# Two-block graph attention on one core: normalised rows split in SBUF and transposed by DMA, maxima on TensorE, merged aggregation jobs, new step orders

## The chip, the cores and the metric

The kernel runs on one core of a Trainium2 chip. The metric is the device time of one execution in microseconds, the median of several. One execution of the same program was also recorded by the hardware profiler; its span, from the first to the last instruction, is what the trace shows.

## The reference

For each of 32 graphs (256 nodes, 384 features, a boolean adjacency matrix) two residual blocks are computed:

```
h = relu(layernorm(x)); x = x + attention6(h, adj)      # 6 heads of 64, scores q k' / 8, masked softmax, @ Wf + bf
h = relu(layernorm(x)); x = x + gat12(h, adj)           # 12 heads of 32

gat12: hv = h W;  s = tanh(hv) w_src;  d = tanh(hv) w_dst
       p = softmax(mask(leaky_relu(s_n + d_m)));  o = elu(p hv + b);  g = sigmoid(h H_w' + H_b)
       result = g * o + (1 - g) * h
```

Everything is float32 to the outside.

## The kernel before

Every engine has its own list of steps in `ORDERS`, written out by hand as text, and `walk` goes through that list once per iteration n. A step has a letter for its lag: L works on graph n+2, P on n+1, A on n, B on n-1, C on n-2. So five graphs are under way together. Between engines only semaphores order the work, so an engine may run ahead of the iteration that another one is in. SyncE (SP) has a list of its own: it waits in order for what each DMA needs, and then issues it.

The weight matrices and the normalised rows are used as two fp16 parts each (high and low), with three products (`TERMS`). A graph goes through these steps, in the names of the lists:

- STATS0 (VectorE: mean and variance), RSTD0 and NORM0 (GpSimd: the normalised rows `xn`, 128 rows x 2 x 384 in float32).
- LN_T0 (L450): TensorE transposes `xn` in six blocks of 128x128 into two PSUM banks (index 0: four blocks, index 1: two). ScalarE takes the high part out with a Relu (L647), VectorE the low part (L844). The result is `h16`, the features on the partitions.
- Q, K (L476), V (L462): projections. QK (L511): scores; SCORES0 (VectorE, L879): mask and row minimum; EXP0 (ScalarE, L672); NORMP0 (VectorE reciprocal L886, GpSimd product L1076); PT0 (L535): TensorE transposes the probabilities, and ScalarE copies them out (L679). PV0 (L553): aggregation, in three jobs, one for each pair of heads; ScalarE and VectorE take its two fp16 parts (L684, L891). OUT0 (L462, VectorE L899): output projection and residual.
- STATS1, AGGREGATE1, RSTD1, NORM1, LN_T1: the same for the second block. HEADS and GATE (L462; L458 adds a bias in GATE): projections. ScalarE takes tanh (L690) and a copy (L691).
- SCORE_PROD (GpSimd, L1098 twice and L1104), SCORE_SUM (VectorE, L911 to L922), DST_T (L587, VectorE L926): the destination scores as rows. DST (L526) spreads them for two heads, SCALED (ScalarE, L703) multiplies them by 0.2. Twelve units follow: SCORES1 (VectorE, two L945 and two L951 each), EXP1 (ScalarE, L715), PT1 (L535, ScalarE L723).
- PV1 (L597): aggregation in three jobs; VectorE copies each out (L957). OUT_T (L605) transposes back; ELU_BIAS, ELU_RELU, ELU_EXP, FINISH, SKIP_H, GATES, SKIP, OUT_SUM and STORE make and store the output rows.

Jobs share three PSUM banks in turn (`Jobs`). MASK0 and MASK1 turn the loaded adjacency into masks on GpSimd; LOAD_ADJ of a graph waits until MASK1 has read the same buffer two graphs before.

At the start, ScalarE sums each weight's absolute values per partition (L623), GpSimd takes the maximum over the partitions (`partition_all_reduce`, L1009), VectorE makes scales, ScalarE the high part (L627) and VectorE the low part (L778). The sums of four weights stand ahead of the first high part on ScalarE. The bias row of the values is made by fp32 products at the very start (L420).

Of the kernel before, what the change touches and what calls it, by code (L numbers as in the profile page):

```python
# [66 lines left out]
def steps(text):  # L67
# [6 lines left out]
        C PT1 9, A QK 0, B GATE 0, A QK 1, C PT1 10, C PT1 11, B GATE 1, P LN_T0 0, A PT0 0, C PV1 2, B DST_T 0,  # L74
        A QK 2, A PT0 1, C OUT_T 0, P LN_T0 1, B DST 0, C OUT_T 1, A PT0 2, A PV0 0, B DST 1, P Q 0, A PT0 3,
        P K 0, P K 1, A PT0 4, P Q 1, A PT0 5, A PV0 1, A PV0 2, B DST 2, B PT1 0, B DST 3, B PT1 1, A OUT0 0,
        B PT1 2, A OUT0 1, B PT1 3, P Q 2, B DST 4, B PT1 4, P V 0, P V 1, B PT1 5, A LN_T1 0, A LN_T1 1, P K 2,
        B PT1 6, B DST 5, A HEADS 0, A HEADS 1, B PT1 7, B PV1 0, B PT1 8, B PV1 1
    """),
    "ACT": steps("""  # L80
        C PT1 8, C EXP1 10, C PT1 9, C EXP1 11, A EXP0 0, B GATE 0, A EXP0 1, C PT1 10, C PT1 11, B GATE 1,
        P LN_T0 0, A EXP0 2, A EXP0 3, A PT0 0, A PT0 1, P LN_T0 1, B SCALED 0, A EXP0 4, A PT0 2, A PV0 0,
        A EXP0 5, B SCALED 1, P Q 0, B EXP1 0, C ELU_RELU 0, A PT0 3, C ELU_EXP 0, A PT0 4, A PT0 5, B EXP1 1,
        A PV0 1, P Q 1, A PV0 2, B SCALED 2, B EXP1 2, B PT1 0, B EXP1 3, B PT1 1, B PT1 2, B SCALED 3,
        B EXP1 4, B PT1 3, B SCALED 4, B PT1 4, P Q 2, B EXP1 5, P V 0, B EXP1 6, P V 1, A LN_T1 0, A LN_T1 1,
        B PT1 5, B EXP1 7, B SCALED 5, B PT1 6, B EXP1 8, A HEADS 0, A HEADS 1, B PT1 7, B EXP1 9
    """),
    "DVE": steps("""
        C SCORES1 10, C SCORES1 11, C PV1 0, A SCORES0 0, C PV1 1, A SCORES0 1, A NORMP0 0, C RECIP1 0,
        A SCORES0 2, A SCORES0 3, A NORMP0 1, B SCORE_SUM 0, P LN_T0 0, A NORMP0 2, C PV1 2, B DST_T 0,  # L90
        B SKIP_H 0, A SCORES0 4, A NORMP0 3, C OUT_T 0, A SCORES0 5, P LN_T0 1, C OUT_T 1, B SCORES1 0, A PV0 0,
        A NORMP0 4, B SCORES1 1, A NORMP0 5, P K 0, B SCORES1 2, P K 1, C FINISH 0, B SCORES1 3, A PV0 1,
        A PV0 2, C FINISH 1, B SCORES1 4, A OUT0 0, B SCORES1 5, A OUT0 1, A STATS1 0, A STATS1 1,
        A AGGREGATE1 0, B SCORES1 6, L STATS0 0, B SCORES1 7, A LN_T1 0, A LN_T1 1, B SCORES1 8, P K 2,
        B SCORES1 9
    """),
    "POOL": steps("""
        B SCORE_PROD 0, A NORMP0 0, A NORMP0 1, B MASK1 0, A NORMP0 2, A NORMP0 3, C ELU_BIAS 0, P MASK0 0,
        A NORMP0 4, A NORMP0 5, C OUT_SUM 0, B GATES 0, A RSTD1 0, A NORM1 0, L RSTD0 0, P RES_ROW 0, B SKIP 0,
        L NORM0 0  # L100
    """),
    "SP": steps("""
        P LOAD_ADJ 0, L LOAD_X 0, C STORE 0
# [1077 lines left out]
```

## Time and profile before

| | |
|---|---|
| median of 3 runs | 1360.45 us (1359.81 to 1360.91) |
| the profiled execution's own time | 1360.17 us |
| its span | 1358.3 us |
| TensorE busy | 1293.0 us, 95% |
| ScalarE busy | 1252.5 us, 92% |
| VectorE busy | 1213.5 us, 89% |
| GpSimd busy | 903.3 us, 66% |
| mean granted TensorE clock | 0.981 |

The profiled execution lies 0.3 us below the median, and its span 1.9 us below its own time. Busy time is a union over an engine's instructions: neighbouring instructions overlap in the pipeline, so the mean duration of one is longer than the distance from its start to the next one's.

### The profile page before, as it was taken

To read this page: it belongs to the slowest core of one execution; us is meant where nothing else is said; L and a number is where in the kernel's file an instruction comes from. 1 tells how busy PE (TensorE), PEld (TensorE's weight loads), DVE (VectorE), ACT (ScalarE), POOL (GpSimd) and SP (SyncE) were. 2 spreads that over 40 slices of the span, in tenths; PEclk is the share of its full clock that TensorE was granted. 3 is DMA by queue.
4 is the path that set the end of the run, shared out by engine and by line. 5 is a ranking of instruction groups with operands and counts; after the bars stand their busy time and mean duration, and the time that the engine had idled before them with its cause. 6 is when DMAs were issued, how large, how long until landed. Compare 5 with 4: busy or idle time off the path is not lost.

```text
span 1358.3 us, 33510 instructions
## 1 busy us (share of the span) xinstructions
PE 1293.0 (95%) x10502; PEld 905.9 (67%) x10502; DVE 1213.5 (89%) x4457; ACT 1252.5 (92%) x3731; POOL 903.3 (66%) x1106
## 2 busy tenths in 40 slices
PE   2789999999999999999999999999999999999974
PEld 1567677767667776766777676677667677767652
DVE  3569999999999999999999999999999999999885
ACT  4469999999999999999999999999999999999986
POOL 3366676667777667777766777766677776667653
PEclk8899999999999999999999999999999999999997
DMA  4000000000000000000000000000000000000000
GB/s 155 13 14 15 20 20 27 27 27 15 27 17 23 27 27 25 17 27 15 25 27 27 17 26 27 13 27 27 27 16 27 27 13 27 27 26 4 13 13 24
DMA packets 29839, 33.75 MB, mean 25 GB/s; under 512 B 10464, under 2 KB 29664, under 8 KB 29664
## 3 DMA queue, kind: packets, MB, share of 16 engines
q1 hardware_dynamic: 29664, 31.62, 7.4%
q8 instruction: 86, 1.41, 0.4%
q14 instruction: 89, 0.73, 0.2%
HBM read 19.03 MB, written 12.58 MB: 23 GB/s over the span
## 4 chain that ended last, share of the span: by engine, by line
PE 89%; ACT 2%; DVE 1%; issue 1%; POOL 1%; POOLq 0%; DVEq 0%; ACTq 0%
PE job L462 26%; PE pt L535 20%; PE job L476 13%; PE unit L511 7%; PE job L597 7%; PE job L553 7%; PE unit L526 3%; PE job L450 3%; PE job L605 2%; PE job L458 1%; ACT p L715 1%; PE job L587 1%; DVE unit L945 0%; POOL prod L1098 0%; ACT pT L723 0%
## 5 line engine op out<-in xcount | busy, mean ns | idle before, releaser
L715 ACT ACTIVATE p<-y,min 128x256 f32<-128x256 f32 x768 | 396.1, 542 | 1.5 <-DVE min L951 1.4
L535 PE MATMUL pt<-ident,p 128*128 128x128 f32 x2304 | 355.6, 280 | 9.7 <-ACT p L715 5.2
L945 DVE SCALAR_TENSOR_TENSOR unit<-unit,s,dst 128x256 f32<-128x256 f32 x768 | 334.8, 481 | 9.4 <-DVE min L951 0.5
L535 PEld LDWEIGHTS pt<-ident,p 128*128 128x128 f32 x2304 | 265.9, 142 | 86.5 <-issue 43.6
L462 PE MATMUL job<-w,h 128*128 128x384 f16 x1728 | 301.8, 326 | 0.7 <-DVE h L844 0.6
L951 DVE CUSTOM_DVE_ANT_0 y<-unit,mask 128x256 f32<-128x256 f32 x768 | 291.0, 415 | 0.0
L1076 POOL TENSOR_SCALAR p<-p,rec 128x256 f32<-128x256 f32 x384 | 188.3, 507 | 88.3 <-DVE rec L886 82.6
L462 PEld LDWEIGHTS job<-w,h 128*128 128x128 f16 x1728 | 166.5, 98 | 104.7 <-issue 0.8
L723 ACT ACTIVATE pT<-pt 128x512 f32<-128x512 f32 x384 | 232.1, 626 | 1.2 <-PE pt L535 1.1
L672 ACT ACTIVATE p<-y,min 128x256 f32<-128x256 f32 x384 | 191.2, 505 | 36.6 <-PE pt L535 28.1
L476 PE MATMUL job<-h,w 128*128 128x256 f16 x1728 | 216.7, 274 | 1.4 <-DVE h L844 1.4
L879 DVE CUSTOM_DVE_ANT_0 y<-unit,mask 128x256 f32<-128x256 f32 x384 | 144.4, 420 | 45.3 <-issue 30.3
L476 PEld LDWEIGHTS job<-h,w 128*128 128x128 f16 x1728 | 167.6, 98 | 24.9 <-issue 1.8
L715 ACT ACTIVATION_READ_ACCUMULATOR p<-y,min 128x1 f32 x768 | 179.9, 234 | 0.0
L1136 POOL TENSOR_TENSOR y<-y,xskip 128x768 f32<-128x768 f32 x32 | 58.1, 1817 | 171.4 <-DVE y L982 171.4
L679 ACT ACTIVATE pT<-pt 128x512 f32<-128x512 f32 x192 | 111.5, 602 | 11.8 <-PE pt L535 11.7
L703 ACT ACTIVATE dst<-unit 128x512 f32<-128x512 f32 x192 | 118.5, 618 | 2.0 <-PE unit L526 1.7
L511 PE MATMUL unit<-kT,qT 64*128 64x256 f32 x768 | 110.8, 408 | 4.9 <-DVE min L879 4.9
L462 PE MATMUL job<-w,c 128*128 128x384 f16 x576 | 104.2, 327 | 1.0 <-DVE c L891 1.0
L597 PE MATMUL job<-pT,hv 128*32 128x256 f32 x1536 | 103.7, 388 | 0.7 <-ACT pT L723 0.7
L553 PE MATMUL job<-pT,vv 128*64 128x256 f32 x768 | 98.5, 392 | 0.0
L1130 POOL TENSOR_TENSOR o<-o,gat_b_row 128x768 f32<-128x768 f32 x32 | 58.3, 1823 | 52.9 <-DVE o L968 52.9
(109 smaller groups left out, 2239.9 us busy)
## 6 DMA issues: line engine op xcount, KB each, us to landing
xb<-in_x_dram SPq DMA_DIRECT2D x32, 384.0 KB, 3.4
out_dram<-y SPq DMA_DIRECT2D x32, 384.0 KB, 2.5
pT<-in_w_all_dram SPq DMA_DIRECT2D x4, 576.0 KB, 9.7
adj_raw<-in_adj_dram SPq DMA_DIRECT2D x32, 64.0 KB, 1.9
prod<-in_w_all_dram SPq DMA_DIRECT2D x1, 576.0 KB, 5.2
p<-in_w_all_dram SPq DMA_DIRECT2D x1, 576.0 KB, 9.9
out_row<-in_bf_dram SPq DMA_DIRECT2D x1, 192.0 KB, 4.3
gate_b_row<-in_gate_b_dram SPq DMA_DIRECT2D x1, 192.0 KB, 5.8
```

What stands on the lines that cost most here:

```text
L462: last = mm(bank[:, 0:H], rows[:, i, c, t * P:(t + 1) * P], w16[:, w, j, c, :], start=n == 0, stop=(c, i, j) == (NC - 1, *TERMS[-1]))
L476: last = mm(bank[:, 0:T], w16[:, w, i, c, p * P:(p + 1) * P], h16[0][:, j, c, :], start=n == 0, stop=n == 3 * NC - 1)
L511: last = mm(unit_ps[(2 * p + hh) % 3][:, qt * T:(qt + 1) * T], qT[par][r, p, qt * P:(qt + 1) * P], kT[par][r, p, :], start=True, stop=True)
L535: last = nc.tensor.transpose(pt_ps[u % 2][:, (2 * hh + kt) * P:(2 * hh + kt + 1) * P], probs[:, u % 3, hh, kt * P:(kt + 1) * P], ident[:])
L553: last = mm(bank[D0 * hh:D0 * (hh + 1), 0:T], vv[par][:, kt, h * D0:(h + 1) * D0], pT0[:, p % 2, hh, kt, :], start=kt == 0, stop=kt == NT - 1)
L597: last = mm(bank[D1 * q:D1 * (q + 1), 0:T], hv[par][:, kt, h * D1:(h + 1) * D1], pT1[:, g % 2, q, kt, :], start=kt == 0, stop=kt == NT - 1 ...
L672: last = op(p0[:, u % 3, hh, :], y0[:, u % YB, hh, :], ACT.Exp, bias=min0[:, u, hh:hh + 1], scale=-1.0, accum_out=sum0[:, u, hh:hh + 1])
L715: last = op(p1[:, u % 3, hh, :], y1[:, u % YB, hh, :], ACT.Exp, bias=min1[:, u, hh:hh + 1], scale=-1.0, accum_out=sum1[:, t, h:h + 1])
L723: op(pT1[:, g % 2, q_:q_ + 2, :, t * P:(t + 1) * P], pt_ps[u % 2][:].rearrange("p (h k q) -> p h k q", h=2, k=NT), ACT.Copy).then_inc(s_pT, 1)
L945: V.scalar_tensor_tensor(leaky[:, hh * T:(hh + 1) * T], bank[:, hh * T:(hh + 1) * T], s8[par][:, t, h:h + 1], dst5[:, c % 2, hh, :], ALU.a ...
L951: last = V.tensor_tensor_reduce(y1[:, u % YB, hh, :], leaky[:, hh * T:(hh + 1) * T], mask1[:, t, :], 1.0, 3.0e38, ALU.add, ALU.min, min1[: ...
L1076: last = G.tensor_scalar(p0[:, u % 3, hh, :], p0[:, u % 3, hh, :], rec0[:, u, hh:hh + 1], 1.0, ALU.mult, ALU.mult)
```

## The change

- LN_T0 and LN_T1 go, on all three engines. GpSimd's NORM0 and NORM1 get one more instruction each: Relu of the whole `xn` (128x768) into the fp16 high part `hrow`. A new VectorE step LOW0 or LOW1 makes the low part in rows (one 128x768 instruction from SBUF). A new SP step PARTS_T 0 or 1 waits for it and for the last reader of `h16` of the graph before, and issues two DMA transposes (one for each half of the rows, 128 x 768 fp16 each) into `h16`. Q 0 and HEADS 0 wait for them on TensorE.
- PV0 and PV1 become two jobs each: the first holds two thirds and fills a bank (512 columns), the second holds the last third. `pT0` gets a third buffer.
- The maxima of the weights: a TensorE transpose of the sums, a maximum and a copy on VectorE, and a small TensorE product in place of GpSimd's reduction.
- The setup is cut up and moved: only WQ and WK stand ahead of the first graph; the others' high and low parts, the value bias row, the scaling of rows and the gate's bias follow behind steps of graph 0.
- All five lists of orders are new.

```diff
-        P LOAD_ADJ 0, L LOAD_X 0, C STORE 0
+        P LOAD_ADJ 0, P PARTS_T 0, L LOAD_X 0, A PARTS_T 1, C STORE 0
...
+            def parts_t(b, par, k):
+                done = n_split[k].after(b, f"LOW{k}")
+                if b.ref >= 1:
+                    _, made, _, value = job(b.back(1), *last_reader(b.back(1), k))
+                    read = value
+                sp.wait_ge(s_split[k], done)
+                if b.ref >= 1:
+                    sp.wait_ge(made, read)
+                for t in range(NT):
+                    sp.dma_start_transpose(
+                        h16[k][:, :, :, t * P:(t + 1) * P].rearrange("p j c t -> p (j c) t"),
+                        hrow[k][:, t].rearrange("p j n -> p (j n)")).then_inc(s_hT[k], 16)
...
+            def rows_in_parts(b, k, s_norm, n_norm, step):
+
+                normal = n_norm.after(b, step)
+                pool.wait_ge(s_norm, normal)
+                G.tensor_scalar(hrow[k][:, :, 0, :], xn[k][:], 0.0, 1.0, ALU.max, ALU.mult).then_inc(s_hrow[k], 1)
...
+            def low_rows(k):
+                def part(b, par, _):
+                    dve.wait_ge(s_hrow[k], n_hrow[k].after(b, f"NORM{k}"))
+                    V.scalar_tensor_tensor(hrow[k][:, :, 1, :], xn[k][:], 0.0, hrow[k][:, :, 0, :],
+                                           ALU.max, ALU.subtract).then_inc(s_split[k], 1)
...
+                if t == 0:
+                    pe.wait_ge(s_hT[1], transposed(b))
+                bank, made = bank_free(b, "HEADS", t)
...
+                if (step, p) == ("Q", 0):
+                    pe.wait_ge(s_hT[0], transposed(b))
+                bank, made = bank_free(b, step, p)
```

The new lists of TensorE, VectorE and GpSimd:

```
PE:   A DST 0, P PT0 2, A DST 1, L Q 0, L K 0, P PT0 3, L K 1, P PT0 4, A DST 2, P PT0 5, P PV0 0, P PV0 1,
      A PT1 0, A DST 3, A PT1 1, P OUT0 0, P OUT0 1, A PT1 2, L K 2, A PT1 3, A PT1 4, L V 0, A PT1 5, L V 1,
      A DST 4, L Q 1, A PT1 6, A PT1 7, L Q 2, A DST 5, A PV1 0, A PT1 8, P HEADS 0, P HEADS 1, A PT1 9,
      P GATE 0, L QK 0, A PT1 10, A PT1 11, L QK 1, A PV1 1, P GATE 1, L PT0 0, L QK 2, A OUT_T 0, L PT0 1,
      P DST_T 0, A OUT_T 1
DVE:  A STATS1 1, C FINISH 0, A AGGREGATE1 0, B SCORES1 6, B SCORES1 7, P K 2, A LOW1 0, C FINISH 1,
      B SCORES1 8, L STATS0 0, A SKIP_H 0, B SCORES1 9, B PV1 0, B SCORES1 10, L LOW0 0, B SCORES1 11,
      P SCORES0 0, P SCORES0 1, B RECIP1 0, P SCORES0 2, P NORMP0 0, P SCORES0 3, P NORMP0 1, B PV1 1,
      A SCORE_SUM 0, P NORMP0 2, P SCORES0 4, B OUT_T 0, A DST_T 0, P NORMP0 3, P SCORES0 5, B OUT_T 1,
      A SCORES1 0, P NORMP0 4, P NORMP0 5, A SCORES1 1, L K 0, A SCORES1 2, L K 1, A SCORES1 3, P PV0 0,
      P PV0 1, A SCORES1 4, A SCORES1 5, P OUT0 0, P OUT0 1, P STATS1 0
POOL: L RSTD0 0, L NORM0 0, A SCORE_PROD 0, A MASK1 0, P NORMP0 0, P NORMP0 1, P NORMP0 2, P NORMP0 3,
      A GATES 0, P NORMP0 4, P NORMP0 5, P RES_ROW 0, B ELU_BIAS 0, L MASK0 0, A SKIP 0, P RSTD1 0, P NORM1 0,
      B OUT_SUM 0
```

## Rows read from the trace of the kernel before

**Rows 1.** Windows: length, busy of each engine (instructions), granted clock, DMA share, GB/s.
```profile
0.00:50.00 50.00, 18.98 (x98) 12.99 (x100) 24.12 (x63) 20.50 (x32) 14.12 (x28) 0.83 0.34 105
...
703.48:743.23 39.75, 39.75 (x330) 28.00 (x328) 37.27 (x138) 38.54 (x117) 27.97 (x34) 1.00 0.07 23
```

**Rows 2.** Chain of work, one iteration: start us, us, what.
```profile
703.48 2.92 PE job L462 x18
706.40 0.44 PE pt L535 x4
706.84 0.66 PE job L450 x6
...
714.14 1.00 PE job L597 x16
715.15 0.59 PE pt L535 x4
715.73 1.06 PE unit L511 x8
716.80 0.27 PE job L458
...
722.24 0.44 PE job L450 x4
...
726.31 0.22 PE job L450 x2
726.53 0.22 PE unit L526 x2
726.75 0.33 PE job L605 x3
```

**Rows 3.** Groups by line and form: busy us, mean ns of one, idle before.
```profile
L844 DVE SCALAR_TENSOR_TENSOR h<-job,h 128x512 f16<-128x512 f32 x64 | 44.0, 687 | 16.5 <-ACT h L647 13.9
L647 ACT ACTIVATE h<-job 128x512 f16<-128x512 f32 x64 | 37.9, 592 | 8.9 <-PE job L450 8.9
L982 DVE SCALAR_TENSOR_TENSOR y<-o1m,gate 128x768 f32<-128x768 f32 x32 | 30.3, 948 | 0.0
L844 DVE SCALAR_TENSOR_TENSOR h<-job,h 128x256 f16<-128x256 f32 x64 | 26.7, 417 | 0.2 <-ACT h L647 0.2
L647 ACT ACTIVATE h<-job 128x256 f16<-128x256 f32 x64 | 24.3, 380 | 0.0
L1115 POOL TENSOR_SCALAR gate<-gtanh 128x768 f32<-128x768 f32 x32 | 26.7, 833 | 0.0
```

**Rows 4.** Timeline, steady part: start us, us, engine, line, what.
```profile
743.41 0.85 DVE L945 SCALAR_TENSOR_TENSOR unit<-unit,s,dst 128x256 f32<-128x256 f32 x2
...
744.86 1.01 DVE L819 BATCH_NORM_STATS2 bn<-xb 128x6 f32<-128x384 f32 x2
...
743.58 0.19 POOL L1038 TENSOR_SCALAR nmean<-mv 128x2 f32<-128x2 f32 x1 [1.77 <-DVE mv L813]
...
744.92 1.32 POOL L1068 TENSOR_SCALAR xn<-x,nmean,rstd 128x384 f32<-128x384 f32 x2
...
754.28 1.84 POOL L1098 TENSOR_TENSOR prod<-th,src_row 128x768 f32<-128x768 f32 x1
...
740.23 0.38 SPq L406 DMA_DIRECT2D out_dram<-y  x1
```

**Rows 5.** DMA issues: KB each, us to landing; then the queue's share.
```profile
xb<-in_x_dram SPq DMA_DIRECT2D x32, 384.0 KB, 3.4
out_dram<-y SPq DMA_DIRECT2D x32, 384.0 KB, 2.5
...
adj_raw<-in_adj_dram SPq DMA_DIRECT2D x32, 64.0 KB, 1.9
...
q1 hardware_dynamic: 29664, 31.62, 7.4%
```

**Rows 6.** Timeline of the start.
```profile
31.63 7.16 PE L476 MATMUL job<-h,w 128*128 128x256 f16 x45 [1.41 <-DVE h L844]
```

More of the change, by code:

```diff
@@ L52 @@
 TERMS = ((0, 0), (0, 1), (1, 0))
-JOBS = {"LN_T0": 1, "Q": 1, "K": 1, "V": 1, "PV0": 1, "OUT0": 1, "LN_T1": 1, "HEADS": 1, "GATE": 1,
+HALVES = ((0, 1), (2,))
+JOBS = {"Q": 1, "K": 1, "V": 1, "PV0": 1, "OUT0": 1, "HEADS": 1, "GATE": 1,
         "DST_T": 1, "PV1": 1, "OUT_T": 1}
@@ L73 @@
     "PE": steps("""
[L74 to L78, printed above, removed]
+        A DST 0, P PT0 2, A DST 1, L Q 0, L K 0, P PT0 3, L K 1, P PT0 4, A DST 2, P PT0 5, P PV0 0, P PV0 1,
@@ L82 @@
[L82 to L86, printed above, removed]
+        P EXP0 2, A GATE 0, A GATE 1, P PT0 0, P EXP0 3, P EXP0 4, A SCALED 0, P PT0 1, P EXP0 5, A SCALED 1,
@@ L90 @@
[L90 to L94, printed above, removed]
@@ L232, in build @@
         xn = [sb(f"xn{i}", [P, NT, H]) for i in range(2)]
+        hrow = [sb(f"hrow{i}", [P, NT, 2, H], F16) for i in range(2)]
         h16 = [sb(f"h16_{i}", [P, 2, NC, T], F16) for i in range(2)]
@@ L311, in build @@
         s_q, n_q = sem("s_q_in_sbuf"), Count(NB, "ACT", {"Q": 1})
-        s_hi0, n_hi0 = sem("s_high_part0"), Count(NB, "ACT", {"LN_T0": 1, "PV0": 1})
-        s_hi1, n_hi1 = sem("s_high_part1"), Count(NB, "ACT", {"LN_T1": 1})
+        s_hi0, n_hi0 = sem("s_high_part0"), Count(NB, "ACT", {"PV0": 1})
+        s_hrow, n_hrow = ([sem(f"s_high_rows{i}") for i in range(2)],
+                          [Count(NB, "POOL", {f"NORM{i}": 1}) for i in range(2)])
+        s_split, n_split = ([sem(f"s_parts_in_rows{i}") for i in range(2)],
+                            [Count(NB, "DVE", {f"LOW{i}": 1}) for i in range(2)])
+        s_hT = [sem(f"s_parts_transposed{i}") for i in range(2)]
         s_qk, n_qk = sem("s_scores0"), Count(NB, "PE", {"QK": 1})
@@ L406, in store @@
                 sp.dma_start(out_b, y[:]).then_inc(s_out, 16)
-            walk(sp, ORDERS["SP"], {"LOAD_X": load_x, "LOAD_ADJ": load_adj, "STORE": store}, {-2: load_others})
+            walk(sp, ORDERS["SP"], {"LOAD_X": load_x, "LOAD_ADJ": load_adj, "STORE": store,
+                                     "PARTS_T": parts_t}, {-2: load_others})
             sp.wait_ge(s_out, 16 * NB)
@@ L982, in finish @@
                     V.scalar_tensor_tensor(y[:], o1m[:], -1.0, gate[par][:], ALU.add, ALU.mult).then_inc(s_fin, 1)
-            walk(dve, ORDERS["DVE"], {"STATS0": stats0, "LN_T0": ln_t0,
+            walk(dve, ORDERS["DVE"], {"STATS0": stats0,
                        "K": k_, "SCORES0": scores0, "NORMP0": normp0, "PV0": pv0, "OUT0": out0,
-                       "STATS1": stats1, "AGGREGATE1": aggregate1, "LN_T1": ln_t1,
+                       "STATS1": stats1, "AGGREGATE1": aggregate1,
                        "SCORE_SUM": score_sum, "DST_T": dst_t, "SCORES1": leaky1,
-                       "PV1": pv1, "RECIP1": recip1, "OUT_T": out_t, "FINISH": finish, "SKIP_H": skip_h})
+                       "PV1": pv1, "RECIP1": recip1, "OUT_T": out_t, "FINISH": finish, "SKIP_H": skip_h,
+                       "LOW0": low_rows(0), "LOW1": low_rows(1)})
         @block.gpsimd
@@ L1059, in norm1 @@
                 if b.ref >= 1:
-                    _, made, _, value = job(b.back(1), "LN_T1", 1)
-                    used = value
+                    moved = transposed(b.back(1))
+                if b.ref >= 1:
                     kept = n_hskip.after(b.back(1), "SKIP_H")
```

331 lines of the change are left out of this document (183 added, 148 removed).

## Prediction

> **What bounds the kernel now.** I read the windows first. In one iteration of the steady part [rows 1] TensorE is busy for 39.75 of 39.75 us at the full granted clock (1.00, that is 2.4 GHz), ScalarE for 38.54, VectorE for 37.27, GpSimd for 27.97. So an iteration is as long as TensorE's own list. The reader is to see that the other two are close behind: room for 1.2 and 2.5 us. The chain of waits says the same: a gapless row of TensorE pieces, of which those here [rows 2] are a part. The first 50 us hold 31.0 us of TensorE idleness [rows 1]. A saving on TensorE therefore counts 32 times, as long as neither a busy engine nor a loop of waits becomes longer.
>
> **What the change takes from TensorE.** LN_T0 costs 0.44 + 0.22 and LN_T1 0.66 us: 1.32 us an iteration [rows 2]. A second, smaller term: a transpose group of 4 takes 0.44 us, but 0.59 behind PV1, which uses 32 columns of the array, and a 1.06 us QK is followed by 0.27 us for L458; some 0.13 us is lost wherever narrow products (PV0, PV1, QK) hand over to full ones. I count seven such places an iteration before and five in the new list, which sets PV0 0 beside PV0 1 and QK 1 beside PV1 1: 0.27 us. With both, 38.15 us an iteration. The products themselves stay as many.
>
> **ScalarE and VectorE.** ScalarE loses the Relus: 2 x (592 + 380) ns = 1.94 us by durations [rows 3]; since neighbours overlap I take 1.5 us, which leaves 37.0. Merged PV0 copies save next to nothing. VectorE loses 2 x (687 + 417) ns and gets two instructions of the size of L982, 2 x 948 ns [rows 3]: 0.3 us saved, and two smaller merges 0.1 to 0.2. It has 36.8 us of work in 38.15. GpSimd gets two more of the kind of L1115, 1.67 us, and stands at 29.7: covered. Were that cover gone, it would be 1.67 us. So by load TensorE stays the bound, with 1.1 us of room on ScalarE and 1.3 on VectorE, tighter than before on VectorE.
>
> **The new wait.** The transposes leave the engines, but each parts transfer now has a latency D, from LOW ready to both halves landed, and it lies in two loops that close once an iteration. Both sums are made from starts and durations of the trace.
>
> Loop 1 (second block): LOW1 ready, D, HEADS 0. On TensorE from HEADS 0 to the next DST 0, by the pieces [rows 2]: HEADS 2.92, GATE 2 x (0.27 + 1.46, half of the 2.92 piece), QK 3 x 1.06, PV1 1 1.00, PT groups 5 x 0.44 and 0.14 for a handover, OUT_T 2 x 0.33 with 0.15, DST_T 0.22: 13.9. DST 0 (0.22 [rows 2]) and SCALED, a ScalarE instruction of 512 columns like the 592 ns one [rows 3]: 0.85 with the hand-over. Then VectorE from SCORES1 0 to the next LOW1: eight units of 1.45 (distance of the starts 743.41 and 744.86 [rows 4]), 0.4 for two back-to-back pairs; FINISH 0 and LOW1 1.8, by L982; PV0 0.94, by the two forms of L844 less their overlap [rows 3]; STATS1 with AGGREGATE1 1.2 (a pair of statistics is 1.01 [rows 4]); and by width, between 0.4 and 0.55 each, three K and two OUT0, 2.4, with two short NORMP 0.2: 18.6. Beside its last stretch GpSimd needs 0.08 + 2.66 us for RSTD1 and NORM1 (743.58 to 746.24 [rows 4]) and 0.83 for the high part, as long as the two units and K 2 that cover it (3.6): 0.1 more. The loop is 33.45 + D.
>
> Loop 2 (first block): SP's list puts LOAD_ADJ ahead of PARTS_T 0, and LOAD_ADJ waits for MASK1, which stands behind SCORE_PROD on GpSimd, which waits for the tanh of HEADS. So LOW0, ready long before, does not decide. HEADS 2.92, tanh 0.6, SCORE_PROD 5.5 (three instructions like the 1.84 us one [rows 4]), MASK1 0.7 (two thirds of the width of L1115 [rows 3]), issue of the adjacency 0.5 (0.38 [rows 4] and the wait), D, and TensorE from Q 0 to the next HEADS 0, which is its iteration less the 13.9 above and the 1.1 from DST 0 to Q 0, 23.1: 33.3 + D. Behind PARTS_T on SP stand LOAD_X, PARTS_T 1 and STORE; LOAD_X serves a graph three iterations on, and the store has its own iteration of room.
>
> So the iteration stays TensorE's as long as D is at most 4.7 us, is as long as before at D = 6.3, and every microsecond above 4.7 costs 32.
>
> **How large is D?** No transpose by DMA is in the trace. From below: the same 384 KB leave SBUF in 2.5 us [rows 5], and the second issue adds 0.4 (0.38 [rows 4]): 2.9. From above: if each run of 256 bytes costs what an average packet (1.07 KB) costs now, 0.074 x 16 x 1358.3 / 29664 = 54 ns on its engine [rows 5], the 1536 runs of both halves take 1536 x 54 / 16 = 5.2 us, and with a fixed 1.9 (the 64 KB adjacency, whose 256 runs have that very length [rows 5]) and the second issue 7.5. I take 3.8: 1.9 fixed, 0.4 for the second issue, 1.5 for the other 320 KB at the rate by which 384 KB from HBM exceed 64 KB (3.4 - 1.9 [rows 5]). It is nearest to the adjacency's row, which has the same piece length.
>
> The loads of the trace show that bulk moves fast in this queue [rows 5]. The Trainium skill (VectorE: DVE Perf Modes, "The three transpose paths") gives 1309 ns for one 128x128 block through the DMA crossbar, against 390 ns on TensorE. No run here shows that yet; twelve blocks one after another would be 15.7 us by it, which would give D = 15.7, an iteration of 49.2 and a total near 1650 us. The Trainium skill (DMA: Bandwidth & Descriptors, "Latency and other measured facts") has 261 GB/s, by which the 384 KB would take 1.5 us and the sum would stand. That each block is served alone is a rival below.
>
> **The start.** The first Q runs at 31.63 us [rows 6], behind the sums and high parts of four weights. New: WQ and WK alone stand ahead; I put their scales near 11 us and x, statistics, normalising and low parts near 16, an estimate; but the transposes stand behind six weights in the same queue, 3.4 MB, which at about 0.23 MB/us (320 KB in 1.5 us [rows 5]) end near 16 to 19. Q 0 can start at 20 to 22, 10 us earlier. What is cut up (value bias product, later weights, gate bias) is still to be done in the next iterations, so I give back 3: 7 us gained, bounds 0 to 14. At the end nothing new: the last graph's units and the chain of ELU and store are as long as before.
>
> **The sum.** 1360.2 (the profiled execution's time; the median of the runs is 0.3 above) - 32 x (1.32 + 0.27) = 50.9 - 7 + 1 for what the tight lists will lose at the joints: 1303 us.
>
> **Rivals.**
> - A: as above, TensorE the bound, 1290 to 1318 us. For it: gapless TensorE before, and room of 0.9 us in both loops at D = 3.8. Chance 0.50.
> - B: the new lists don't fit gaplessly. VectorE has 36.8 us of work and ScalarE 37.0 in 38.15; a VectorE step that waits for TensorE has little to catch up with. If an iteration is 38.6 to 39.4, the time is 1318 to 1343. For it: each loop passes through three engines whose waits I added up only along two paths. Against: before, ScalarE ran at 97% without holding TensorE up. Chance 0.23, some of it with D of 5 to 6 (39.0 there).
> - C: D decides. Above 6.5 us (6.3, and 0.2 for the start's 7 us over 32 iterations) the kernel is slower; at the upper bound of 7.5 an iteration is 40.95, 1.2 more than before, and the time 1360 + 38 - 7 = 1391. TensorE would idle before HEADS 0 or Q 0. Chance 0.16.
> - D: transposes served block by block, the mechanism by which twelve blocks each pay on the scale of a transfer's fixed 1.9 us [rows 5]: even at half of that, D is above 11, an iteration 45, the time over 1500. Chance 0.04.
> - E: gain and loss meet, D of 6.2 to 6.5, or a start that loses what the rest gains: 1357 to 1363. Chance 0.03.
> - The remaining 0.04 lies between B and E, 1343 to 1357.
>
> **How the numbers follow.** The likeliest is A, at 1303; its own range is 1290 to 1318. For 8 in 10 the range must take in B and the part up to E: 1290 to 1355, which leaves out C and D (0.20). Within 0.2% of before, which is about what a measurement of this kernel can tell from no change: 0.03. Faster by more: 0.50 + 0.23 + 0.04 = 0.77. Slower by more: 0.16 + 0.04 = 0.20.
>
> **What the changed profile would show.** Right: no L450 group; TensorE busy again for the whole of an iteration of 38 to 38.4 us in the windows; DMA transposes in pairs that land in 3 to 4.5 us; ScalarE near 37 us, VectorE near 36.8; first Q near 21 us. Wrong by D: TensorE's idle time before L462 or L476 with the DMA of `h16` as its releaser, and a landing time of more than 5 us. Wrong by B: small idle pieces before DST or PT on TensorE, released by VectorE or ScalarE. Wrong at the start: a first Q later than 25 us because the transposes are queued behind the weights, or a long idle stretch between graphs 0 and 1. I would be wrong in a way not foreseen if GpSimd's extra instructions made NORM late, or if the transposes took the SBUF's ports from VectorE and lengthened its instructions.

## The result and the profile after

The changed kernel takes 1550.01 us (median of 4 runs, 1543.84 to 1558.06), the one before 1360.68 us beside it: a ratio of 1.1396, 95% interval 1.1369 to 1.1423. It is slower by 189 us, where 1303 us was predicted. The profiled execution is the longest of the four, 1558.06 us.

The windows over 200 us of the steady part come first: length, busy time of TensorE, its weight loads, VectorE, ScalarE and GpSimd with their instructions, granted clock, DMA share, GB/s.

```profile
600.00:800.00 200.00, 177.70 (x1400) 125.94 (x1398) 166.22 (x598) 165.60 (x490) 147.11 (x161) 0.95 0.16 37
```

Before, TensorE had no idle time at all [rows 1]. Now no engine is busy for more than 89% of the stretch, and the granted clock is 0.95. So no engine bounds the kernel; a chain of waits does. The page's chain says so as well:

```profile
PE 23%; DVE 22%; POOL 22%; issue 15%; ACT 15%; DMA 1%; SPq 0%; POOLq 0%; DVEq 0%; ACTq 0%
```

GpSimd, busy for 70% of the span, holds 22% of the chain, and the transposes (DMA) 1%. The groups by line and form show what is in it (busy us, mean ns of one | idle time before them, and what ended it):

```profile
L1109 POOL TENSOR_SCALAR hrow<-xn 128x768 f16<-128x768 f32 x64 | 178.1, 2783 | 5.6
...
L556 PE MATMUL unit<-kT,qT 64*128 64x256 f32 x768 | 146.8, 513 | 97.9 <-DVE unit L1007 94.4 <-DVE min L923 3.6
...
L958 DVE SCALAR_TENSOR_TENSOR hrow<-xn,hrow 128x768 f16<-128x768 f32 x64 | 105.9, 1654 | 134.8 <-POOL hrow L1109 134.8
```

GpSimd's high part, which the prediction put at 0.83 us after L1115 [rows 3], takes 2.78 us. VectorE waits for it for 134.8 us in all, and its own low part, expected at 0.95, takes 1.65 on average.

The chain over one iteration (start, us, engine, what) shows how the pieces hang together:

```profile
714.37 0.68 issue
...
715.91 0.73 POOL rstd L1102
716.74 1.32 POOL xn L1135 x2
718.13 2.79 POOL hrow L1109
...
721.83 0.95 DVE y L1045
722.78 0.80 DVE unit L1007 x2
724.25 0.94 DVE bn L878 x2
...
727.12 1.31 POOL xn L1119 x2
728.51 2.79 POOL hrow L1109
731.36 2.44 issue
733.80 0.88 DVE unit L1007 x2
734.82 2.08 PE unit L556 x8
736.90 1.90 PE pt L586 x8
738.79 1.96 PE unit L556 x8
...
743.92 1.06 PE unit L556 x8
```

And the timeline of the same place, with the idle time before an instruction and its releaser in brackets:

```profile
720.95 0.96 DVE L958 SCALAR_TENSOR_TENSOR hrow<-xn,hrow 128x768 f16<-128x768 f32 x1 [2.10 <-POOL hrow L1109]
...
721.93 2.54 SPq L435 DMA_TRANSPOSE h<-hrow  x2
...
731.26 1.80 POOL L1168 TENSOR_TENSOR prod<-th,src_row 128x768 f32<-128x768 f32 x1
731.33 2.55 DVE L958 SCALAR_TENSOR_TENSOR hrow<-xn,hrow 128x768 f16<-128x768 f32 x1 [1.89 <-POOL hrow L1109]
733.02 2.52 POOL L1168 TENSOR_TENSOR prod<-th,dst_row 128x768 f32<-128x768 f32 x1
...
734.82 2.08 PE L556 MATMUL unit<-kT,qT 64*128 64x256 f32 x8 [3.55 <-DVE unit L1007]
```

The reader is to see four things. Both blocks' high parts lie on one chain, because VectorE's list sets STATS0 of the next graph behind LOW1 of this one: 718.13 and 728.51. The low part of the first block lies beside GpSimd's two-input products L1168 and takes 2.55 us instead of 0.96; the second product, which begins before it ends, takes 2.52 instead of 1.8. By these rows the two engines seem to take turns: the first product keeps its 1.80 us, the low part ends 0.8 us behind it, and the second product 1.7 us behind the low part. (The chain calls this stretch, 731.36 to 733.80, issue.) SCORES1 11 stands behind it, and TensorE's QK 0 waits 3.55 us for the bank that this step frees. After that wait the pieces run at the lower of the two clocks (1.2 GHz): QK 2.08 and 1.96 us, eight transposes 1.90, where the same view has 1.06 for QK at 743.92 and [rows 2] give 0.44 for four transposes. That is (2.08 - 1.06) + (1.96 - 1.06) + (1.90 - 0.88) = 2.9 us by clock alone. The windows row of those pieces gives the granted clock, 0.51:

```profile
734.80:740.70 5.90, 5.88 (x26) 4.03 (x27) 2.23 (x13) 3.56 (x11) 3.17 (x3) 0.51 0.21 43
```

This is one of the dearer iterations. In the next, after a wait of 3.51 us, the first QK takes 2.03 us and the second 1.13 again. The average is smaller than 2.9 us, and the run with the copy below gives it.

The transposes answer to [rows 5]; the columns are the median us from issue to landing, and then packets, MB and share of the queue:

```profile
h<-hrow SPq DMA_TRANSPOSE x128, 2.8
...
q1 hardware_dynamic: 132064, 56.80, 16.3%
```

Each of a pair lands 2.8 us after its issue, and an issue takes 1.27 us (2.54 for two, above): D = 1.27 + 2.8 = 4.1 us, where 3.8 was taken.

The start, on TensorE (timeline):

```profile
21.05 2.08 PE L521 MATMUL job<-h,w 128*128 128x256 f16 x9 [10.79 <-DMA h<-hrow]
...
62.26 5.92 PE L507 MATMUL job<-w,c 128*128 128x384 f16 x18 [3.75 <-DVE c L941]
...
78.17 3.90 PE L521 MATMUL job<-h,w 128*128 128x256 f16 x18 [6.03 <-DVE kT L902]
87.62 5.25 PE L507 MATMUL job<-w,h 128*128 128x384 f16 x18 [5.55 <-issue]
```

The first Q stands at 21.05 us, 10.6 earlier than in [rows 6]. At OUT0 of graph 0 it is 4.5 us (62.26 against 66.80 in the trace before), and it is lost behind that: TensorE waits for steps of graph 0 between which setup work now lies, and runs this OUT0 at the lower clock (granted 0.50), 5.92 us where the same piece takes 3.08 at 113.30.

The stores put the difference in three parts. In the trace before, the first output store is issued at 144.03 and the 29th at 1256.99, so one iteration is 39.75 us. After, they are at 171.28 and 1458.63: 45.98 us. With the spans 1358.3 and 1556.3: 27.3 us are lost before the first store, 28 x 6.23 = 174.4 in the steady part, and 3.6 are gained behind it; the sum is the 198.0 us between the spans. The question for the experiments is the 6.2 us in an iteration.

### The profile page after: what moved, and what is told of

It is laid out like the page before. It is cut to its first block, busy times and chain, and to the rows that moved or that the text cites. A ratio compares the mean times of both kernels' runs of the same rounds, so it can differ in the third digit from the quotient of the medians.

```text
span 1556.3 us, 32567 instructions
## 1 busy us (share of the span) xinstructions
PE 1314.4 (84%) x10127; PEld 918.2 (59%) x10127; DVE 1237.5 (80%) x4335; ACT 1223.4 (79%) x3571; POOL 1096.3 (70%) x1168
## 4 chain that ended last, share of the span: by engine, by line
PE 23%; DVE 22%; POOL 22%; issue 15%; ACT 15%; DMA 1%; SPq 0%; POOLq 0%; DVEq 0%; ACTq 0%
POOL hrow L1109 11%; PE unit L556 9%; DVE unit L1007 7%; PE pt L586 6%; PE job L507 4%; ACT p L762 4%; DVE y L1013 4%; ACT p L715 4%; POOL rstd L1102 3%; POOL xn L1135 3%; ACT pT L725 2%; POOL xn L1119 2%; ACT dst L750 2%; DVE x L952 2%; PE job L649 2%
## 5 line engine op out<-in xcount | busy, mean ns | idle before, releaser
L762 ACT ACTIVATE p<-y,min 128x256 f32<-128x256 f32 x768 | 385.9, 513 | 149.4 <-DVE min L1013 149.3
L586 PE MATMUL pt<-ident,p 128*128 128x128 f32 x2304 | 366.7, 291 | 78.1 <-ACT p L762 41.9
L586 PEld LDWEIGHTS pt<-ident,p 128*128 128x128 f32 x2304 | 283.9, 150 | 155.7 <-ACT p L762 80.3
L770 ACT ACTIVATE pT<-pt 128x512 f32<-128x512 f32 x384 | 219.4, 603 | 70.1 <-PE pt L586 69.2
L556 PE MATMUL unit<-kT,qT 64*128 64x256 f32 x768 | 146.8, 513 | 97.9 <-DVE unit L1007 94.4
L958 DVE SCALAR_TENSOR_TENSOR hrow<-xn,hrow 128x768 f16<-128x768 f32 x64 | 105.9, 1654 | 134.8 <-POOL hrow L1109 134.8
L715 ACT ACTIVATE p<-y,min 128x256 f32<-128x256 f32 x384 | 190.4, 500 | 22.4 <-PE pt L586 13.3
L1109 POOL TENSOR_SCALAR hrow<-xn 128x768 f16<-128x768 f32 x64 | 178.1, 2783 | 5.6
L556 PEld LDWEIGHTS unit<-kT,qT 64*128 64x128 f32 x768 | 89.4, 241 | 130.0 <-issue 123.1
L762 ACT ACTIVATION_READ_ACCUMULATOR p<-y,min 128x1 f32 x768 | 156.5, 204 | 0.0
L1099 POOL TENSOR_SCALAR nmean<-mv 128x2 f32<-128x2 f32 x64 | 18.6, 290 | 149.2 <-DVE mv L872 149.2
L725 ACT ACTIVATE pT<-pt 128x512 f32<-128x512 f32 x192 | 109.6, 590 | 2.7 <-PE pt L586 2.3
```

The costliest lines, as they stand in the source:

```text
L556: last = mm(unit_ps[(2 * p + hh) % 3][:, qt * T:(qt + 1) * T], qT[par][r, p, qt * P:(qt + 1) * P], kT[par][r, p, :], start=True, stop=True)
L586: last = nc.tensor.transpose(pt_ps[u % 2][:, (2 * hh + kt) * P:(2 * hh + kt + 1) * P], probs[:, u % 3, hh, kt * P:(kt + 1) * P], ident[:])
L715: last = op(p0[:, u % 3, hh, :], y0[:, u % YB, hh, :], ACT.Exp, bias=min0[:, u, hh:hh + 1], scale=-1.0, accum_out=sum0[:, u, hh:hh + 1])
L762: last = op(p1[:, u % 3, hh, :], y1[:, u % YB, hh, :], ACT.Exp, bias=min1[:, u, hh:hh + 1], scale=-1.0, accum_out=sum1[:, t, h:h + 1])
L770: op(pT1[:, g % 2, q_:q_ + 2, :, t * P:(t + 1) * P], pt_ps[u % 2][:].rearrange("p (h k q) -> p h k q", h=2, k=NT), ACT.Copy).then_inc(s_pT, 1)
L1109: G.tensor_scalar(hrow[k][:, :, 0, :], xn[k][:], 0.0, 1.0, ALU.max, ALU.mult).then_inc(s_hrow[k], 1)
```

## The experiments

### The instructions by themselves

A small kernel issues the disputed instructions one by one, twice each, with VectorE idle; then VectorE's two parts beside a GpSimd product. It computes nothing of the reference. An assumption until then was that the fp16 output made GpSimd slow.

> Instructions measured by themselves; the rest of the kernel is left out (the output is a copy of x). Theory H (writing fp16 is what makes GpSimd's high part 2.78 us): GpSimd's 128x768 instruction takes 0.83 us with a float32 target whatever the operations are, and 2.5 to 2.9 us with an fp16 or bf16 target whatever the operations are, the copy too. Rival O (the maximum is what is slow): 2.8 us for the maximum with a float32 target and 0.83 us for multiply-add with an fp16 target. Second question, why VectorE's low part takes 0.96 us in one step and 2.55 in the other: if the neighbour on GpSimd does it, the low part takes 0.96 alone and over 2 us beside GpSimd's tensor_tensor; if not, 0.96 both times. A pair of DMA transposes lands about 4.1 us after its first issue (1.27 + 2.8).

Groups by line and form. L236 to L241 are in turn maximum, affine (times, plus), maximum, affine, maximum (into bf16) and maximum over half the width, and L242 a copy; L266 and L269 are VectorE's parts beside L245, L262 and L261 the same alone:

```profile
L245 POOL TENSOR_TENSOR tt_out<-src,other 128x768 f32<-128x768 f32 x6 | 12.8, 2130 | 4.4 <-DVE high_beside L263 4.0
L266 DVE SCALAR_TENSOR_TENSOR low_beside<-src,high_dve 128x768 f16<-128x768 f32 x3 | 7.5, 2489 | 2.1 <-POOL tt_out L245 2.1
L236 POOL TENSOR_SCALAR f_max<-src 128x768 f32<-128x768 f32 x2 | 5.5, 2774 | 43.9 <-DMA src<-in_x_dram 43.8
L238 POOL TENSOR_SCALAR f_max<-src 128x768 f16<-128x768 f32 x2 | 5.5, 2772 | 0.2
...
L269 DVE TENSOR_SCALAR high_beside<-src 128x768 f16<-128x768 f32 x2 | 4.1, 2040 | 0.1
...
L262 DVE SCALAR_TENSOR_TENSOR low_alone<-src,high_dve 128x768 f16<-128x768 f32 x2 | 1.9, 959 | 0.1
...
L239 POOL TENSOR_SCALAR f_affine<-src 128x768 f16<-128x768 f32 x2 | 1.7, 831 | 0.2
L242 POOL CAST f_copy<-src 128x768 f16<-128x768 f32 x2 | 1.6, 824 | 0.1
L261 DVE TENSOR_SCALAR high_dve<-src 128x768 f16<-128x768 f32 x2 | 1.1, 560 | 70.0 <-POOL f_copy L242 70.0
```

The output's type does nothing: the maximum takes 2.77 us into fp32 and into fp16, the affine form 0.83 into both. The theory of the slow fp16 output fell, and its rival, the operation, stood. The same question put to the whole kernel, with the maximum written in float32 into spare tiles, has no time: each of them needs 3072 bytes of SBUF on a partition, and 1568 were free. A second small kernel put other forms of the same instruction at those places:

> Instructions by themselves; the rest of the kernel is left out (the output is a copy of x). Theory M (any maximum or minimum in GpSimd's tensor_scalar puts it on a slow path of about 3.5 ns an element and partition row): 2.8 us for 128x768 with the maximum first, second or alone, with minimum too, 0.83 us only without; a comparison with zero is open. Rival P (only this pair, maximum then multiply, is slow): 0.83 us for at least one of the other forms. Second question: VectorE's low part beside a GpSimd instruction with one input (copy). If it is two-input instructions on GpSimd that take VectorE's port, the low part takes 0.96 us here, against 2.5 beside tensor_tensor; if any GpSimd instruction does it, 1.3 or more.

A maximum alone took 2.13 us, as did a comparison (is_gt); multiply then maximum, add then maximum, maximum then add, and minimum then multiply took 2.78. So every maximum, minimum and comparison that was tried is slow on GpSimd in this instruction, and multiply-add and copies are not. Here GpSimd copied beside VectorE, and the low part took 1.50 us, the high part 1.06.

### The high part taken from GpSimd

Three versions of the changed kernel, all with its lists. In the first VectorE makes the high part in LOW0 and LOW1:

```diff
+    V.tensor_scalar(hrow[k][:, :, 0, :], xn[k][:], 0.0, 1.0, ALU.max, ALU.mult).then_inc(s_hrow[k], 1)
...
-    G.tensor_scalar(hrow[k][:, :, 0, :], xn[k][:], 0.0, 1.0, ALU.max, ALU.mult).then_inc(s_hrow[k], 1)
```

> The high part is made by VectorE just ahead of the low part (one more instruction of about 0.55 us in each of the two steps, as SKIP_H's), and GpSimd's instruction goes. Theory H: VectorE has 1.0 us more work an iteration (36.9 + 1.0 = 37.9 in 38.15), GpSimd's normalising is the only thing that VectorE waits for, an iteration of 38.5 to 40.5 us, time 1310 to 1375, and a chance to beat the kernel before. Rival L: above 1450. Rival S: the low part of the first block still meets GpSimd's tensor_tensor, 1.6 us an iteration lost, 1360 to 1420.

1379.96 us (1376.05 to 1381.58), ratio 1.0138 [1.012, 1.0156], 40.1 us from store to store. In the second ScalarE makes it with a Relu (new steps HIGH0 and HIGH1, 0.85 us each):

> The high part is made by ScalarE (Relu of 128x768 into fp16, 0.85 us each, in list places where the normalised rows should just be there), and GpSimd's instruction goes. ScalarE then has 37.0 + 1.5 = 38.5 us of work and becomes the bound with TensorE. Theory H: an iteration of 38.7 to 41 us, 1315 to 1390. Rival L: above 1450. Rival S: 1380 to 1440.

1383.82 us (1382.26 to 1386.08), ratio 1.0171 [1.0154, 1.0188], 40.0 us. They take 170 and 166 of the 189 us away, though they give 1.1 and 1.7 us an iteration to an engine that had little room by the prediction's count; in the second ScalarE is busy for 192.67 us of 200. The first lies 5 us above the range of its theory, the second in it. The third leaves GpSimd's instruction in its place and makes a copy of it. The Relu of the high part is left out, and that is all that its output lacks:

```diff
-    G.tensor_scalar(hrow[k][:, :, 0, :], xn[k][:], 0.0, 1.0, ALU.max, ALU.mult).then_inc(s_hrow[k], 1)
+    G.tensor_copy(hrow[k][:, :, 0, :], xn[k][:]).then_inc(s_hrow[k], 1)
```

> The changed kernel with GpSimd's maximum-and-multiply (2.78 us) replaced by a copy of the same 128x768 elements into the same fp16 tile (0.83 us, what the prediction had put in). The Relu of the high part is left out, so values differ slightly; every other instruction is there. Theory M (the 1.95 us per instruction, twice an iteration, is what the changed kernel lost, through VectorE's waits): an iteration of 38.3 to 39.6 us, 1305 to 1350, faster than before. Rival L (the loops through the DMA transposes are too long as well): 39.7 to 41 us, 1360 to 1400. Rival S (low part beside GpSimd's tensor_tensor): 39.7 to 40.5, with low parts of 2.5 us in the profile.

1365.64 us (1364.87 to 1366.37), ratio 1.0042 [1.0028, 1.0056]. The windows, the two groups, and all idle time of TensorE between 700 and 746 us:

```profile
600.00:800.00 200.00, 193.63 (x1593) 136.56 (x1591) 184.26 (x676) 187.82 (x559) 148.00 (x181) 1.00 0.20 43
```

```profile
L958 DVE SCALAR_TENSOR_TENSOR hrow<-xn,hrow 128x768 f16<-128x768 f32 x64 | 61.1, 955 | 12.1 <-POOL hrow L1109 9.2
...
L1109 POOL CAST hrow<-xn 128x768 f16<-128x768 f32 x64 | 52.6, 822 | 4.0
```

```profile
706.30 0.63 PE L586 MATMUL pt<-ident,p 128*128 128x128 f32 x4 [0.88 <-ACT pT L770]
...
725.54 1.13 PE L556 MATMUL unit<-kT,qT 64*128 64x256 f32 x8 [0.31 <-DVE min L923]
...
745.77 0.41 PE L586 MATMUL pt<-ident,p 128*128 128x128 f32 x2 [0.88 <-ACT pT L770]
```

This is the pricing of the one instruction: 1.96 us less in each of two places of an iteration (2.78 to 0.82) took 184 of the 189 us away. The iteration came out at the upper end of its theory's range, the time 16 us above it and in rival L's. The clock is back at 1.00, the low parts are at 0.955 us (nothing of GpSimd's products is beside them any more), and the wait of 3.55 us is gone. An iteration is 39.57 us (160.65 to 1268.59 in 28).

The windows over these 28 iterations, in the changed kernel and with the copy, part the loss into work and waiting:

```profile
171.28:1458.63 1287.35, 1133.98 (x8848) 799.40 (x8848) 1064.13 (x3753) 1055.34 (x3110) 953.59 (x1008) 0.95 0.17 37
```

```profile
160.65:1268.59 1107.94, 1076.05 (x8856) 757.82 (x8852) 1023.89 (x3753) 1044.83 (x3109) 825.08 (x1008) 1.00 0.19 43
```

TensorE is busy for 40.5 us an iteration in the one and 38.4 in the other, with the same pieces but for eight at the edges; so of the 6.4 us, 2.1 are its lower clock and 4.3 are idle time.

Then the maximum was put back in one block at a time (a copy in the other; that block's Relu of the high part is left out):

> The slow form of the high part (2.78 us) in the first block only; the second block has the 0.83 us copy (without Relu). Against the run with both copies (39.56 us an iteration, 1365.6 us): theory W (the late high part makes VectorE wait at LOW0, and LOW0 then meets GpSimd's tensor_tensor and takes 2.5 us, and QK 0 waits behind it with a fallen clock): 2 to 5 us an iteration more, 1430 to 1530, low parts of the first block of 2.5 us. Rival A (the two slow forms simply add, 1.95 us each, no amplification): 41.5 us an iteration, 1428. Rival N (the first block has slack, only the second counts): under 0.5 us an iteration more.

> The slow form in the second block only. My loop 1 has RSTD1, NORM1 and the high part in it and about 0.8 us of slack at HEADS 0, so theory W: 1.95 less 0.8 or so, 1 to 2 us an iteration more, 1400 to 1430, TensorE waiting ahead of HEADS 0. Rival A: 1.95, 1428. Rival N': most of the changed kernel's loss sits here, 4 us an iteration or more, over 1490.

With it in the first block alone 1463.4 us (1462.95 to 1467.38), ratio 1.0771 [1.0753, 1.0789]; in the second alone 1419.3 (1418.62 to 1421.27), ratio 1.044 [1.0424, 1.0455]. Both lie in the ranges of their theories W. The low part's group of each, first block and then second:

```profile
L958 DVE SCALAR_TENSOR_TENSOR hrow<-xn,hrow 128x768 f16<-128x768 f32 x64 | 104.5, 1633 | 71.4 <-POOL hrow L1110 65.7 <-POOL hrow L1112 2.1
```

```profile
L958 DVE SCALAR_TENSOR_TENSOR hrow<-xn,hrow 128x768 f16<-128x768 f32 x64 | 61.2, 956 | 75.8 <-POOL hrow L1110 68.7 <-POOL hrow L1112 7.1
```

VectorE waits alike in both, 66 and 69 us. But only in the first block does the low part slip under the products (1633 ns on average), and that block costs 98 us, 3.1 an iteration, against 54 us, 1.7, in the second. The second's is a little under its 1.96 us; the first's exceeds it by 1.1, and its low parts are longer by 2 x (1.633 - 0.955) = 1.4 us.

Where TensorE stands idle for it differs too. The first block's shows before QK, for the bank that SCORES1 11 frees (76.0 us in all, none of it in the run with the copy). The second block's was expected ahead of HEADS, at the transposes, and 8 us more are there (10.5 against 2.5 us). But 33 us more are before PT1, as in this iteration, where TensorE waits for probabilities whose scores VectorE makes behind LOW1:

```profile
659.25 0.66 PE L586 MATMUL pt<-ident,p 128*128 128x128 f32 x4 [1.10 <-ACT p L762]
```

Together the two are 151 of the 184 us; the rest, 1.0 us an iteration, comes only with both. From store to store they are 3.2 and 1.7 us, and 6.4 with both; TensorE's busy time in it rises by 0.8, 0.4 and 2.1. So most of what only both cost (0.9 of 1.5 us by this count) is the lower clock. With the first alone TensorE waits 2.87 us or less before QK, and in many iterations the clock stays at 1.00 behind it:

```profile
646.80:650.00 3.20, 3.20 (x24) 2.25 (x24) 2.20 (x13) 2.49 (x7) 3.03 (x3) 1.00 0.02 5
```

### What is left when GpSimd is fast

1365.64 us is still slower than before. Three runs looked for a wait in the loops, all with the copy. The first sets LOW0 ahead of SCORES1 10 on VectorE:

> As the run before, with LOW0 one step earlier in VectorE's list (ahead of SCORES1 10), where GpSimd's tensor_tensor has not begun. Rival S: 1 to 1.6 us an iteration faster than the run before (30 to 50 us in all). Theory M: no more than 0.5 us an iteration either way, since the normalised rows are then not there yet.

1386.12 us (1384.87 to 1386.87), ratio 1.019 [1.0175, 1.0205]: 20 us worse, where one side expected 30 to 50 us less and the other at most 16 us either way. Moved up, the low parts wait 48.8 us in all for GpSimd's part, against 9.2 before the move. GpSimd's part is ready just in time for LOW0's old place (720.36 us against 720.42 in the trace of the run with the copy) and no sooner. The second adds a third transpose ahead of the second block's pair, 1.22 us of the queue (its output is read by nobody):

> As the run with the copy, with one more DMA transpose (into a spare tile) ahead of the two of the second block: HEADS 0 gets its rows 1.27 us later. If the loop through the second block's transposes sets the iteration (rival L), the time is 1.27 us an iteration more than that run, 41 us in all. If it has room (my loops: 4.7 us allowed, 4.1 measured), under 0.7 us an iteration, 22 us in all.

1397.12 us (1391.43 to 1400.7), ratio 1.0268 [1.024, 1.0296], with 24.8 us of waiting for `h` before HEADS (2.5 without it). That is 31.5 us more than without, 1.0 us an iteration for 1.2 us added. The prediction's loop 1 (33.45 + 4.1 = 37.6 us) would have had 2.0 us of room in an iteration of 39.57 and shown nothing. The extra transpose also holds up the store behind it in SP's list, so not all of the 31.5 us need be loop 1; the 22 us more before HEADS are.

The third moves ScalarE's PT1 0 ahead of ELU_EXP, since the longest wait that TensorE has left, 0.88 us, is for ScalarE's copy of PT1. A fourth run adds to it the low part of WG and the gate's bias behind LOW1 of graph 0:

> The run with both copies, with ScalarE's PT1 0 one step earlier in its list (ahead of ELU_EXP 0). There TensorE stood 0.88 us an iteration ahead of PT1 2, released by that copy. Theory J (the lists lose at single joints, each worth its wait): 0.4 to 0.9 us an iteration less, 1337 to 1353, faster than the kernel before. Rival K (the wait only moves to another joint, since ScalarE and VectorE are nearly full): within 0.2 us an iteration, 1359 to 1372.

> As the run before, with VectorE's low part of the gate weight and the gate bias chain (5 us and more) moved behind LOW1 of graph 0, out of the path to its HEADS. If these pieces of setup hold up graph 0, 4 to 8 us in all; if not (the first iterations wait for something else), under 2 us.

1365.9 us (1364.82 to 1368.29), ratio 1.0047 [1.0032, 1.0062], and 1364.28 (1363.61 to 1366.4), ratio 1.0034 [1.002, 1.0047]. In the first the wait is 0.83 us and at another PT1: it moved and hardly shrank, as its rival had it (its theory: 1353 us at most). In the second the first store is issued at 156.78 instead of 159.28, and 1.6 us of these 2.5 are left at the end, under 2 as expected if the first iterations wait for something else.

### Part of the change in the kernel before

Was the scheme itself sound? The last runs start from the kernel before, with its own lists and its four-bank jobs. Only the first block's LN_T0 goes: VectorE makes the high and the low part in rows, and SP transposes them by DMA. The whole reference is computed.

```diff
-        B SCORE_SUM 0, P LN_T0 0, A NORMP0 2,
+        B SCORE_SUM 0, P LOW0 0, A NORMP0 2,
...
-        P LOAD_ADJ 0, L LOAD_X 0, C STORE 0
+        P LOAD_ADJ 0, L LOAD_X 0, P PARTS_T 0, C STORE 0
```

> The kernel before with its own orders and its own four-bank jobs; only the first block's four fp32 transpositions on TensorE are replaced: VectorE makes the high part (0.56 us alone) and the low part (0.96 alone) in rows, and two DMA transposes bring them across. GpSimd gets nothing new. Theory (the scheme is sound where GpSimd has no maximum in it): TensorE loses 0.66 us in an iteration (0.44 + 0.22 for the two pieces), so 32 x 0.66 = 21 us less at best, and the start moves by at most 6 us either way: 1335 to 1348 us. Rival (the second list of steps has no room for the transposes' 4.1 us and for VectorE's slower low part, 1.5 us beside a GpSimd copy): the first Q projection of the iteration waits for them, the 0.66 us is given back, and the time is 1358 us or more, with TensorE's idle time at Q 0 put down to the DMA.

1397.27 us (1393.31 to 1399.72), ratio 1.027 [1.0252, 1.0287]. The rival stood. First the group, then its first piece from the timeline:

```profile
L493 PE MATMUL job<-h,w 128*128 128x256 f16 x1728 | 220.4, 277 | 48.4 <-DMA h<-hrow 48.2
```

```profile
34.36 6.86 PE L493 MATMUL job<-h,w 128*128 128x256 f16 x45 [15.03 <-DMA h<-hrow]
```

Of the 48.2 us of waiting, 15.0 are before the first Q of all; the other 33.2 us are 1.1 an iteration (not the 1.5 that the next two expectations start from), against the 0.66 taken from TensorE. The first store is 8.7 us later than before (152.74 against 144.03), and an iteration takes 40.73 us, 1.0 more. Two runs took that wait down. LOW0 works in halves of the rows, and each half's transpose is issued as soon as it is there; in one of the two, TensorE's list also has A PT0 3 ahead of P Q 0:

```diff
+                for t in range(NT):
+                    V.tensor_scalar(hrow[:, t, 0, :], xn[0][:, t, :], 0.0, 1.0, ALU.max, ALU.mult).then_inc(s_hrow, 1)
...
+                    V.scalar_tensor_tensor(hrow[:, t, 1, :], xn[0][:, t, :], 0.0, hrow[:, t, 0, :],
+                                           ALU.max, ALU.subtract).then_inc(s_split, 1)
```

> As the run with Q 0 later, but TensorE's list is that of the kernel before (P Q 0 ahead of A PT0 3). Theory: the wait at Q 0 falls from 1.5 us by the 0.75 us that the first transpose goes off earlier, and the time is 1397 - 32 x 0.75 = 1373 us, within 7 us either way. Rival: the four half instructions cost VectorE more (0.2 us) and the second transpose waits for its own half, so that nothing is gained: 1393 us or more.

> The kernel before with only the first block's transpositions by DMA, and LOW0 cut into the two halves of the rows (high 0, low 0, high 1, low 1), each half's transpose issued as soon as it is there; besides, TensorE's list has A PT0 3 (0.44 us) ahead of P Q 0. With one LOW0 and the old order TensorE waited 1.5 us in an iteration for the transposes (the time was 1397 us). Theory (the wait at Q 0 is only a matter of the place in the lists, and TensorE's 0.66 us come back once it is gone): the first transpose goes off 0.75 us earlier and Q 0 0.44 us later, 0.3 us of the wait are left, and the time is 1397 - 32 x 1.2 = 1359 us, within 7 us either way. Rival (TensorE's list was a loop in balance with VectorE and ScalarE, so that the freed time and the delays come back as other waits): TensorE's idle time moves to QK, DST or PT, and the time stays above 1375 us.

By halves 1387.04 us (1383.87 to 1393.38), ratio 1.0203 [1.0176, 1.0231]; with Q 0 later 1380.16 (1379.12 to 1383.55), ratio 1.0158 [1.0144, 1.0173]. The first lies between its theory (1380 at most) and its rival (1393 or more), the second in its rival's range. The wait before the Q and K products fell from 48.2 to 28.8 and 19.7 us (of which 14.8 and 14.2 are before the first Q of all), so 19 and 29 us less, and the time by 10 and 17: a bit more than half of it came back. TensorE's joints in one iteration of the last show where the rest went (timeline):

```profile
692.70 1.07 PE L608 MATMUL job<-pT,hv 128*32 128x256 f32 x16
693.91 0.29 PE L598 MATMUL job<-ident_b,nd_parts 128*36 128x128 bf16 x2
...
696.03 0.55 PE L616 MATMUL job<-ident,oT 128*128 128x128 f32 x3 [0.18 <-DVE oT L971]
...
702.76 0.66 PE L546 MATMUL pt<-ident,p 128*128 128x128 f32 x4 [0.34 <-POOL p L1088]
```

In this iteration nothing waits for the transposes, and yet it takes 40.13 us, 0.38 more than before. Over 28 iterations TensorE is busy for 39.51 us in each and idle for 0.74; so its work fell by 0.24 us and not by the 0.66 of the two pieces, and why not by more was not measured. DST_T starts 1.21 us behind PV1 2 where it was 1.00 in the trace before, OUT_T waits for VectorE's copy, PT0 4 for GpSimd's product, which VectorE's reciprocal starts. VectorE's high and low halves cost 2 x (0.35 + 0.56) = 1.8 us, in one lump, where the two pieces of LN_T0 cost 0.69 + 0.42 = 1.1 [rows 3] in two places. That the lump delays what TensorE needs next from VectorE fits the waits, but no run moved it alone: in the whole run TensorE's idle time is 5.1 us before DST_T, 6.3 before OUT_T and 19.7 before the transposes of PT0 and PT1, where the trace before has 1.1, 0.9 and 9.7.

## Why the prediction was wrong

- **The step that failed** is the term for GpSimd: "GpSimd gets two more of the kind of L1115, 1.67 us, and stands at 29.7: covered." L1115 is an affine instruction of the same size, but the new one contains a maximum. It measured 2.78 us, not 0.83, and a copy in its place gave 184 of the 189 us back. L1115 was the nearest row by shape and engine, but no row of before has a maximum on GpSimd, and the text put no upper bound in for that.
- The same step's second half, "covered", failed as well. "Were that cover gone, it would be 1.67 us" priced the loss as the load of the two instructions. But VectorE, which works through its list in order, waits for each of them at LOW1 and LOW0, and everything behind LOW in that list is late with it; so its length is paid about once a block. It also pushed LOW0 under GpSimd's products (0.96 to 2.55 us) and TensorE's QK into the lower clock (2.9 us in the iteration shown, 2.1 on average). By averages 2 x 1.96 + 1.4 + 2.1 = 7.4 us, of which 6.4 remain in the iteration (45.98 against 39.57 with the copy). The transposes are little of it: the chain has 1% for them. The text named "if GpSimd's extra instructions made NORM late" among the ways not foreseen, without a price or a chance, and it was not NORM but the extra instruction itself that was late.
- **D was right**: 4.1 us against 3.8. Rivals C and D were not it: twelve blocks take 4.1 us together. The Trainium skill (VectorE: DVE Perf Modes, "The three transpose paths") has 1309 ns for one 128x128 block; one after another, twelve would be 15.7 us by an estimate from it, and the trace does not agree with that reading.
- **The loads were right** once the copy stands in for the maximum: in the stretch of 200 us, taken to an iteration of 39.57, TensorE is busy for 38.3 us (38.15 predicted), ScalarE for 37.2 (37.0), VectorE for 36.5 (36.8), GpSimd for 29.3 (29.7).
- **The joints were mis-sized**: 1 us for all of them, where the version with the copy idles 1.26 us in each iteration of that stretch (39.57 - 38.3) and 1.14 in each of the 28, mostly before PT1 and QK; that is 36 to 40 us in all. That is the mechanism of rival B, though the 39.57 us lie just above its 38.6 to 39.4. The run with one more transpose lost 1.0 of 1.2 us, where loop 1 by its sum had 2.0 us of room; so the sum is most likely short by 1.5 us or more. Which term of it is too small was not measured.
- **The start**: the first Q was right (20 to 22, measured 21.05), the 7 us of gain wrong. With the copy the first store is issued 16.6 us later than before (160.65 against 144.03), the steady part gains 5.0 (28 x 0.18) and the end 6.3, which makes the 5.3 us between those spans. What was cut up was to be done "in the next iterations", but it lies in the lists of graph 0, which is alone then and has nothing to cover it. Moving two pieces of it gave 2.5 us back at the first store, and ScalarE's PT1 0 one step earlier 1.4. What the other 13 us belong to is open.
- So even with the term for GpSimd right, the forecast would have been some 60 us too low: in the copy's run the other parts of the change make the kernel 0.4% slower. The loads held; the sum over gapless lists did not.
- The runs that start from the kernel before show the general form. TensorE gives 0.66 us a block away by its pieces, VectorE gets 0.4 to 0.7 more, and as VectorE has 2.5 us of room an iteration [rows 1], by load this is free. It was not: 1380 us at best. What is not shown is that no list has room for it; two orders were tried.

## What to carry to other kernels

Before an instruction is costed by a neighbour's row, compare the operation and not only engine, shape and type: on GpSimd a maximum took 2.6 times (alone) to 3.3 times (with a second operation) as long as an affine form of the same size. Where work is taken from the busiest engine and given to others, sum the length of the whole loop in which the new work stands, and not the load of each engine: here 1.96 us there cost 1.7 in one place and 3.1 in the other. A wait can be paid twice, by a lower clock and by work that slips beside something it collides with. When a change with many parts comes out slower, replace one suspected instruction by a cheap one of the same shape: one run priced it.
